# Products of the output projection and of q in other slots of the step: one attention block over a batch of 16 on one core

## What is computed

```python
def _sln(h, w, ln_g, ln_b, Wg, bg, Wb, bb):
    ...
    gamma = (w @ Wg.T + bg)[:, None, :]
    beta = (w @ Wb.T + bb)[:, None, :]
    return gamma * ln + beta
h = _sln(hidden, w, ln_g, ln_b, Wg, bg, Wb, bb)
qkv = (h @ Wqkv.T + bqkv).reshape(B, N, num_heads, hd, 3)
energy = jnp.einsum('bhqd,bhkd->bhqk', q, k)
att = jax.nn.softmax(energy, axis=-1) / D ** 0.5
out = jnp.einsum('bhqk,bhkd->bhqd', att, v)
out = out @ Wp.T + bp
h1 = out + hidden
h2 = _sln(h1, w, ln_g, ln_b, Wg, bg, Wb, bb)
return h2 + h1
```

## Time and profile before

| what | value |
|---|---|
| median of 3 runs | 345.15 us |
| lowest, highest | 345.02, 347.54 us |
| the profiled execution | 345.56 us |
| its span in the trace | 343.8 us |
| TensorE busy | 332.5 us, 97%, 3173 products |
| TensorE weight loads | 286.8 us, 83% |
| VectorE busy | 298.3 us, 87% |
| ScalarE busy | 242.8 us, 71% |
| POOL busy | 159.1 us, 46% |
| granted TensorE clock | 1.0 in all of it |

### The profile page before, as it was taken

The page is one execution under the profiler, slowest core; times in us unless marked ns, Lnnn a source line. Parts: engine busy times, 40 slices in busy tenths (PEclk is TensorE's granted clock), DMA queues, the critical chain, the costliest instruction groups (busy, mean ns, idle before and its releaser), DMA issues.

```text
span 343.8 us, 8981 instructions
## 1 busy us (share of the span) xinstructions
PE 332.5 (97%) x3173; PEld 286.8 (83%) x3173; DVE 298.3 (87%) x728; ACT 242.8 (71%) x476; POOL 159.1 (46%) x187
## 2 busy tenths in 40 slices
PE   8888999999999999999999999999999999999993
PEld 4677879888888988888888988888898988888773
DVE  4888978799898989899898989989898988999684
ACT  7664876868676786868686876868687786766740
POOL 5765544437164545527264644617254643224330
PEclk9999999999999999999999999999999999999999
DMA  7396445456555454555545454655556354652021
GB/s 242 126 218 186 124 115 140 129 155 157 170 141 156 134 152 135 173 156 170 142 125 169 134 155 134 184 142 160 161 135 157 98 157 123 182 146 67 16 61 61
DMA packets 47705, 48.87 MB, mean 142 GB/s; under 512 B 6287, under 2 KB 41374, under 8 KB 47662
## 3 DMA queue, kind: packets, MB, share of 16 engines
q1 hardware_dynamic: 44494, 46.74, 49.2%
q10 hardware_dynamic: 1184, 1.07, 1.2%
q0 software_dynamic: 1984, 0.51, 0.8%
HBM read 9.99 MB, written 4.23 MB: 41 GB/s over the span
## 4 chain that ended last, share of the span: by engine, by line
PE 87%; DVE 5%; DMA 3%; ACT 1%; issue 1%; ACTq 1%; SPq 0%; DVEq 0%
PE m L976 24%; PE st L976 19%; PE sa L976 18%; PE pv L976 17%; PE pv L1065 4%; DVE mx L692 3%; PE pv L1146 2%; PE m L1105 2%; DMA wqkv<-WqkvT_dram 2%; DMA kst<-qk_l 1%; PE pv L1079 1%; PE m L1079 1%; ACT p L602 0%; DVE qk_l L727 0%; ACTq L625 0%
## 5 line engine op out<-in xcount | busy, mean ns | idle before, releaser
L692 DVE TENSOR_REDUCE mx<-sa 128x2 f32<-128x512 f32 x256 | 171.5, 684 | 28.4 <-PE sa L976 27.3
L602 ACT ACTIVATE p<-st 128x512 f32<-128x512 f32 x240 | 140.9, 598 | 37.5 <-PE st L976 33.2
L976 PE MATMUL sa<-kst,qst 126*128 126x256 f32 x512 | 105.6, 288 | 2.0 <-DMA kst<-qk_l 1.0
L976 PE MATMUL st<-qst,kst 128*128 128x256 f32 x496 | 104.1, 292 | 0.2
L976 PEld LDWEIGHTS st<-qst,kst 128*128 128x128 f32 x496 | 75.1, 188 | 13.8 <-issue 12.8
L976 PEld LDWEIGHTS sa<-kst,qst 126*128 126x128 f32 x512 | 78.6, 189 | 4.6 <-DVE mx L692 1.7
L368 POOL DMA_DIRECT2D qst<-m_h x31 | 17.6, 567 | 112.4 <-DVE m_l L701 112.4
L976 PE MATMUL pv<-p,v_st 128*32 128x256 f32 x1008 | 61.0, 382 | 0.0
L976 PEld LDWEIGHTS pv<-p,v_st 128*32 128x32 f32 x1008 | 29.5, 109 | 21.0 <-ACT p L602 1.5
L976 PE MATMUL m<-hT_h,wqkv_h 128*128 128x256 f32 x128 | 36.8, 300 | 1.3 <-ACT hT_h L616 0.7
L377 POOL TENSOR_SCALAR xn<-xa,mv,rstd 128x256 f32<-128x256 f32 x28 | 34.2, 1227 | 1.5
(11 more groups left out here) (149 smaller groups left out, 566.2 us busy)
## 6 DMA issues: line engine op xcount, KB each, us to landing
qst<-qk_h SPq DMA_DIRECT2D x64, 128.0 KB, 2.4
qst<-qk_l SPq DMA_DIRECT2D x64, 128.0 KB, 2.5
kst<-qk_h SPq DMA_DIRECT2D x62, 128.0 KB, 2.5
kst<-qk_l SPq DMA_DIRECT2D x62, 128.0 KB, 2.8
xa<-x_dram SPq DMA_DIRECT2D x16, 256.0 KB, 3.0
gb<-gb_rows SPq DMA_DIRECT2D x16, 256.0 KB, 3.9
out_dram<-y SPq DMA_DIRECT2D x15, 256.0 KB, 3.4
wqkv<-WqkvT_dram SPq DMA_DIRECT2D x1, 512.0 KB, 5.6
```

Of the source, the lines that this page charges most:

```text
L602: nc.scalar.activation(p32[:, h, :], st_ps[h % 2][:], ACT.Exp).then_inc(exp_done, 1)
L692: dve.tensor_reduce(mx[:, par(a), h // HH, (h % HH) * TT:(h % HH + 1) * TT], sa_ps[h % 2][:].rearrange("p (t n) -> p t n", t=TT), AX.X, AL ...
L976: return nc.tensor.matmul(o, l, r, start=start, stop=stop)
```

## The change

The output projection's quarters go from slots 12, 13, 14, 15 to slot 15 and slots 0, 1, 1 of the step behind. There it is the projection of b - 2, and for sequence 13 its last three quarters stand in `last_step`, after the scores of heads 0 and 1. q's products are made in a new order, all that read the high part of h first (`Q_PRODUCTS`): the first six go to slots 12 and 13 of the step in front (there for sequence b + 3), the other six stay in slots 3 and 4. The first waits for hT_h, the ninth for hT_l; before, all of q waited for hT_l. The wait for aTl moves with the first quarter of the projection from slot 12 to 15. No product is added or dropped.

```diff
--- before.py
+++ after.py
@@ -42,7 +42,7 @@
 VC = 2 * HD
 PV_SLOTS = (10, 2)
 
-Q_SLOTS, K_SLOTS, V_SLOTS, P_SLOTS = (0, 1, 3, 4), (4, 5, 5, 6), (7, 7, 8, 8), (12, 13, 14, 15)
+Q_SLOTS, K_SLOTS, V_SLOTS, P_SLOTS = (12, 13, 3, 4), (4, 5, 5, 6), (7, 7, 8, 8), (15, 0, 1, 1)
 S_MT1, S_AT, S_MT0, S_XT = 1, 10, 9, 10
 S_QH, S_KH, S_VH = 5, 7, 9
 WARM = (10, 4, 4, 4)
@@ -53,6 +53,7 @@
 NX = 6
 S_O1, S_O0 = 3, 12
 S_OT1, S_OT0 = 6, 14
+Q_PRODUCTS = [(0, 0, g, k) for g in range(2) for k in range(2)] + [(w, 1 - w, g, k) for w in (1, 0) for g in range(2) for k in range(2)]
 
 
 def cond_block(nc, x, condT, vectors, WgT, WbT, WqkvT, WpT, bp, out):
@@ -990,6 +991,20 @@
                 if quarter == 3:
                     o.then_inc(done, 1)
 
+            def project_q(a, quarter):
+
+                p = par(a)
+                for n in range(3 * quarter, 3 * quarter + 3):
+                    w, low, g, k = Q_PRODUCTS[n]
+                    if n == 0:
+                        wait(pe, hTh_ready, 1 * a + 1)
+                    if n == 8:
+                        wait(pe, hTl_ready, 1 * a + 1)
+                    o = mm(m0[:, g * N:(g + 1) * N], (wqkv_h, wqkv_l)[w][:, k, g * P:(g + 1) * P],
+                           (hT_h, hT_l)[low][:, p, k, :], n == 0, n == 11)
+                if quarter == 3:
+                    o.then_inc(q_done, 1)
+
             def project_v(a, ps, quarter):
 
                 p, t, k = par(a), quarter // KT, quarter % KT
@@ -1188,7 +1203,10 @@
 
             def last_step():
                 last_scores(0)
+                project_out(1)
                 last_scores(1)
+                project_out(2)
+                project_out(3)
                 wait(pe, att_ready, 2 * (B - 2) + 1)
                 transpose_max(B - 1, 1, pv_ps[0])
                 last_scores(2)
@@ -1278,10 +1296,10 @@
                         if first(b):
                             pe.wait_ge(gbrow_ready, 1)
                         transpose_max(b, 1, pv_ps[0])
-                    for quarter in [n for n in range(4) if Q_SLOTS[n] == h and has(b + 2) and not first(b + 1)]:
-                        if quarter == 0:
-                            wait(pe, hTl_ready, 1 * (b + 2) + 1)
-                        project_qk(b + 2, 0, m0, q_done, quarter)
+                    for quarter in [n for n in range(4) if Q_SLOTS[n] == h]:
+                        a = b + 3 if quarter < 2 else b + 2
+                        if has(a) and a > 1:
+                            project_q(a, quarter)
                     for quarter in [n for n in range(4) if K_SLOTS[n] == h and has(b + 2) and not first(b + 1)]:
                         if quarter == 0:
                             wait(pe, h1_ready, 1 * (b - 2) + 1)
@@ -1298,11 +1316,14 @@
                             wait(pe, ql_ready, (1 * (b + 2) + 1) if has(b + 2) else B)
                             wait(pe, v_ready, 1 * b + 1)
                         project_v(b + 1, m0, quarter)
-                    for quarter in [n for n in range(4) if P_SLOTS[n] == h and has(b - 1)]:
-                        if quarter == 0 and first(b - 1):
+                    for quarter in [n for n in range(4) if P_SLOTS[n] == h]:
+                        a = b - 1 if quarter == 0 else b - 2
+                        if not has(a):
+                            continue
+                        if quarter == 0 and first(a):
                             pe.wait_ge(wpl_ready, 1)
                         if quarter == 0:
-                            wait(pe, aTl_ready, 1 * (b - 1) + 1)
+                            wait(pe, aTl_ready, 1 * a + 1)
                             wait(pe, h1_ready, 1 * (b - 2) + 1)
                             wait(pe, kl_ready, (1 * (b + 2) + 1) if has(b + 2) else B)
                             wait(pe, ml_ready, 2 * min(b + 1, B - 1) + 1)
```

## The result

The changed kernel takes 347.97 us, median of 20 runs (346.62 to 350.21), the kernel before, run beside it, 345.5 us (344.96 to 347.86). The ratio is 1.0069, with a 95% interval of 1.0048 to 1.009: slower, by 0.7%, and by 0.9 us more than the forecast's +1.6.

The account below looks back on a forecast made before the run. TensorE was taken to bound the kernel, with 87% of the chain of waits. Start +1.04, steady steps 0, turn +0.38 and last step +0.20 made +1.62 us on 345.15, giving 346.8 us, range 345.0 to 347.8.

Parts of the forecast that it names:

- The start of the batch: Steps -1 to 1: moved q products wait for hT_h and make VectorE late; +1.04 us.
- The turn: Step 13 to 14: nine output products move over, slot 14 gives back 0.35, waits hide 0.33; +0.38 us.
- the gate: What TensorE loses after a wait: a released pair ends 0.56 us after its releaser, one product 0.44, three 0.68.
- The last step: Step 14 gains 0.35 in slot 14; nine products behind mostly fill the transpose's wait for att; +0.20 us.
- the start was not hidden: Rival: hT_h(2) in time or VectorE's lateness made up by step 0; 345.3 us, chance 0.25 in whole or part.
- the gaps were not simply filled: Rival: moved work only fills gaps at start, turn and last step, no gate holds; -1.23 us, 343.9 us, chance 0.06.
- slot 12 shows no wait for hT_h: Rival: slot 12 waits for hT_h in each of 13 steps, 0.14 us each reaches 348.6 us; chance 0.09.
- the steady steps come out at zero: Repeated steps: scores of slots 15, 0 and 1 come 0.35 us earlier, no new gate costs anything; 0 us.
- a step that is not 19.49 us: Sign of being wrong in the changed profile: a steady step should still take 19.49 us.
- 13 x 0.1 = 1.3: Bound on the steady steps: from 0 to 0.1 us lost in each of 13 repeats.
- the edges' 1.62: Forecast sum of start +1.04, turn +0.38 and last step +0.20, with steady steps at 0.
- TensorE's pulled-ahead weight loads: Skill's rule, not used in the sum: a waiting product's weights lie ready, start 0.19 us less, total 346.6 us.

Follow-up runs that it names:

- e2: Changed kernel, but sequence 2's first six q products stay in slots 0 and 1 of step 0; 345.95 us, ratio 1.0027 to the kernel before.
- e6: Changed kernel with sequence 2's first six q products in slots 14 and 15 of step -1; 345.90 us, ratio 0.9995 to the kernel before.
- e4: Kernel before with only slot 14's three output products moved, to slot 1 of the next step, q as before; 344.97 us, ratio 0.9975.
- c1: The changed kernel itself, unaltered, run again on another chip; 347.59 us, ratio 1.0058 to the kernel before.
- s1: The changed kernel itself, unaltered, run in a later call beside variants on one chip; 347.40 us, ratio 1.0045 to the kernel before.
- e8: Changed kernel with sequence 2's q products in slots 14, 15 of step -1 and the output projection left in slots 12 to 15; 348.77 us, ratio 1.0081.
- e5: Kernel before with moves of q and output products only at the batch's start, turn and last step, steady steps as before; 344.58 us, ratio 0.997.

## Why the prediction was right and wrong

**Right, by its steps.** The start of the batch: slot 13's maximum at 32.52 for 32.56, then 1.16, 1.11 and 1.04 us late for 1.11, 1.11 and 1.04, and the gap of 1.02 us ahead of the product at 31.28 is ended by ScalarE's hT_h. e2 and e6 move it away and back. The turn: 0.39 for 0.38; slot 14's scores end at 301.97, 2.03 later than the 299.94 of before, which is all lateness brought from ahead: only their own three products' time came off, as the gate said, and e4 shows the same gate from the other side. The last step: 0.19 for 0.20. The rivals fall with these: the start was not hidden, the gaps were not simply filled, and slot 12 shows no wait for hT_h in a steady step (0.36 us for its three products, as without one).

**Wrong: the step "the steady steps come out at zero".** The list of gates there has hT_h, the exponential of slot 12, att and transposes, the residual, aTl. It has instructions of engines and what SP waits for, but no landing of a transfer. The scores of slot 0, which that same paragraph moves 0.35 us ahead, read qst, into which POOL's transfer puts m_l, and this transfer was looked at in the last step alone ("shows no wait"). In the kernel before, the issue of m_l at 180.45 stands 4.4 us ahead of its reader (184.86); the change makes that about 4.05 (108.42 - 104.35 in the changed kernel's trace gives 4.07). The 13 landings that slot 0 reads in steps 2 to 14 took 2.39 to 4.50 us there (median 3.44). The slowest already cost something. Here are its issue in the timeline, its landing in the list of m_l's transfers, and the pair of scores behind it in the chain, which takes 0.36 us where others take 0.23:

```profile
258.46 0.49 POOL L368 DMA_DIRECT2D qst<-m_l  x1
...
DMA to landing us min/median/max: 4.5/4.5/4.5
...
263.15 0.36 PE st L976 x2
```

So the margin left, 4.05 us, was 0.6 against the usual landing and less than nothing against the slowest, and it was never worked out. The term put at 0 measured 0.99 in the profiled run, 0.83 of it in one wait for m_l. The other 0.16 is spread over the steps (19.53 for 19.49 in the one shown), as is c1's 0.20, and its cause is open. s1's 0.69 has a wait of 0.45 us. Between kernels of one call, the wait is worth 0.4 to 0.5 us. The prediction's own sign of being wrong, a step that is not 19.49 us, came.

**What the bound held.** The steady steps were bounded by 13 x 0.1 = 1.3, which takes in every one of these, but the chances gave 0.09 to 347.5 and up, all of it for another wait (hT_h in slot 12), and the range ended at 347.8. 347.97 lies 0.17 us above that end, and this small excess is partly chance: the forecast was added to a median of 345.15 from three runs, where the kernel before measured 345.50 beside the changed one. Of the miss of 1.2 us (347.97 for 346.8) 0.35 is that. With the edges' 1.62 and 0.5 for m_l the sum against 345.5 is 347.6; the other 0.3 to 0.4 us of the first comparison was not located. Calls differ by as much: 2.52 undisturbed in the first, then 2.24 and 1.77.

**TensorE's pulled-ahead weight loads.** The Trainium skill (TensorE: Matmul & The Clock Gate, Step-by-step: what each phase is for) says that weight loads are pulled ahead of matmuls in flight; read as holding for a waiting product too, it would have put the start 0.19 us lower, by the prediction's estimate. The changed kernel's trace does not show this for the product that waits: its weight load starts at 31.28, behind hT_h's end at 31.23, and the three products take 0.62 from there. The measured start fits the whole gate.

## What to carry to other kernels

Where work is moved so that an instruction comes earlier, list everything that it waits for, transfers included, and hold each margin against the slowest landing of that very transfer in the trace (4.50 us here, for a margin of 4.4), not against the median of all or against whether the list of waits names it today. Products in a loop whose engine is always busy are free to move, but they are cover: count what each slot's products hide (e8: 0.3 us in each step when they are gone). The gain lies at the edges, where the chain leaves the busy engine; e5 moves only there and is 1 us faster.

## What the runs showed of the hardware

A transfer of 8 KB from POOL's queue lands in 1.7 to 4.5 us in the kernel before, and in up to 4.87 in the changed one. Where a load of 256 KB was issued within 1 us ahead of it on SP's queue the median is 3.49 us, where the load came behind 2.66, with none near 2.46 (234 transfers of 18 profiles). The medians move by twice the 0.35 us by which a quarter's products move a reader.

In the long start TensorE's products take nearly twice as long for some 8 us, while the records give the granted clock as 1.00, the level of 2.4 GHz, in every stretch of 5 us up to 25, in s1 as in the kernel before. In s1's timeline, ahead of the first scores:

```profile
6.06 1.89 PE L977 MATMUL pv<-cond,wg 128*128 128x16 f32 x8
...
10.38 1.91 PE L977 MATMUL sa<-zeros 128*128 128x512 bf16 x4
...
23.67 0.50 PE L977 MATMUL sa<-kst,qst 126*128 126x256 f32 x2 [1.07 <-DMA kst<-qk_l]
```

and in the kernel before:

```profile
5.91 1.06 PE L976 MATMUL pv<-cond,wg 128*128 128x16 f32 x8
...
8.19 1.03 PE L976 MATMUL sa<-zeros 128*128 128x512 bf16 x4
...
21.23 0.50 PE L976 MATMUL sa<-kst,qst 126*128 126x256 f32 x2 [1.04 <-DMA kst<-qk_l]
```

The same products take 1.89 and 1.91 us for 1.06 and 1.03, and the first scores start 2.44 us later; from about 14 us on equal products take equal time. What decides which start an execution gets stays open.
